# A two-layer attention and expert kernel on one core: in the second attention, the magnitudes' square roots move from ScalarE to VectorE, the ring of exp tiles grows from 8 to 16, and the bias matmuls go in 256-column steps

## The reference, cut to what matters

```python
xn = _layernorm(x, axis=-1)
# attention: heads of 8 channels; the product with v is elementwise,
# so of the softmax only its sums per query are needed
att = jnp.einsum('blhd,bmhd->blmh', q, k) * scale
att = jax.nn.softmax(att, axis=2)
opt = jnp.einsum('blmh,blhd->blhd', att, v).reshape(b, l, d)
attention = opt @ w_out.T + b_out
# "ffn": the magnitudes
real = jnp.einsum('bti,io->bto', xn, jnp.cos(theta + theta_noise))
imag = jnp.einsum('bti,io->bto', xn, jnp.sin(phi + phi_noise))
x = x + attention + jnp.sqrt(real * real + imag * imag)
```

## Time and profile before

| | |
|---|---|
| median of 3 runs | 1477.16 us |
| span of the profiled execution | 1475.7 us |
| what lies around the span (difference) | 1.5 us |
| second attention's stage | 987 us to the end |
| ACT busy | 98% of the span |
| DVE, PE, POOL busy | 84%, 76%, 43% |

### The profile page before, as it was taken

The page is one execution under the profiler, slowest core; times in us unless marked ns, Lnnn a source line. Parts: engine busy times, 40 slices in busy tenths (PEclk is TensorE's granted clock), DMA queues, the critical chain, the costliest instruction groups (busy, mean ns, idle before and its releaser), DMA issues.

```text
span 1475.7 us, 21637 instructions
## 1 busy us (share of the span) xinstructions
PE 1125.2 (76%) x7910; PEld 441.5 (30%) x7910; DVE 1245.1 (84%) x2236; ACT 1445.4 (98%) x796; POOL 632.5 (43%) x529
## 2 busy tenths in 40 slices
PE   5587786887887988878878774787778677776766
PEld 2122223144252441542524411232123122221212
DVE  6998887988989879789798787858898898998886
ACT  3999999999999999999999999999999999999998
POOL 5166460754509577595585820732113023022100
PEclk8599998999999999999999997899999999999999
DMA  4843544213242212122121321034033033021020
GB/s 124 247 137 74 160 128 124 58 52 85 79 136 65 56 43 58 38 56 64 31 66 48 84 68 31 20 108 93 28 117 76 31 110 82 27 106 34 22 72 19
DMA packets 104061, 112.73 MB, mean 76 GB/s; under 512 B 41722, under 2 KB 76026, under 8 KB 103946
## 3 DMA queue, kind: packets, MB, share of 16 engines
q1 hardware_dynamic: 98618, 99.47, 24.5%
q0 software_dynamic: 4464, 11.09, 2.7%
q10 hardware_dynamic: 864, 0.69, 0.2%
HBM read 66.52 MB, written 44.70 MB: 75 GB/s over the span
## 4 chain that ended last, share of the span: by engine, by line
ACT 72%; issue 12%; DVE 11%; PE 3%; POOL 2%; DMA 1%; SPq 0%; ACTq 0%; DVEq 0%; POOLq 0%
ACT scores L785 28%; ACT scores L746 25%; ACT exp L1304 11%; DVE exp L1312 5%; DVE scores L695 4%; ACT exp L1300 2%; ACT ht L1037 1%; ACT L785 1%; ACT L746 1%; POOL yro L1091 1%; PE pvb L676 1%; PE ring L661 1%; ACT scores L778 0%; PE ring L1279 0%; POOL at L1254 0%
## 5 line engine op out<-in xcount | busy, mean ns | idle before, releaser
L695 DVE TENSOR_SCALAR scores<-ring 128x1024 f32<-128x1024 f32 x512 | 589.7, 1216 | 28.7 <-PE ring L661 23.5
L785 ACT ACTIVATE scores<-scores 128x8192 f32<-128x8192 f32 x63 | 438.9, 7020 | 0.2
L1304 ACT ACTIVATE exp<-ring 128x1024 f32<-128x1024 f32 x438 | 432.7, 1419 | 0.2
L746 ACT ACTIVATE scores<-scores 128x8192 f32<-128x8192 f32 (+1 forms) x59 | 404.2, 6919 | 0.2
L1279 PE MATMUL ring<-stk 128*128 128x512 bf16 x1024 | 306.7, 385 | 122.8 <-ACT exp L1304 100.1
L676 PE MATMUL pvb<-scores,val 128*9 128x256 f32 x4096 | 324.6, 392 | 80.6 <-issue 38.4
L1312 DVE SCALAR_TENSOR_TENSOR exp<-exp 128x512 f32<-128x512 f32 x438 | 322.6, 758 | 62.2 <-ACT exp L1304 56.3
L661 PE MATMUL ring<-stk 64*128 64x512 bf16 x1024 | 210.4, 408 | 56.6 <-DVE scores L695 44.5
L1279 PEld LDWEIGHTS ring<-stk 128*128 128x128 bf16 x1024 | 65.8, 97 | 338.3 <-ACT exp L1304 234.4
L661 PEld LDWEIGHTS ring<-stk 64*128 64x128 bf16 x1024 | 49.9, 93 | 288.5 <-DVE scores L695 201.8
L676 PEld LDWEIGHTS pvb<-scores,val 128*9 128x9 f32 x4096 | 65.6, 89 | 210.8 <-issue 207.4
(11 more groups left out here) (263 smaller groups left out, 1415.8 us busy)
## 6 DMA issues: line engine op xcount, KB each, us to landing
stk<-stack SPq DMA_DIRECT2D x192, 192.0 KB, 2.8
stack<-qp SPq DMA_DIRECT2D x7, 768.0 KB, 4.7
stack<-kp SPq DMA_DIRECT2D x7, 768.0 KB, 5.7
xj<-xg SPq DMA_DIRECT2D x10, 448.0 KB
yg<-xj POOLq DMA_DIRECT2D x10, 448.0 KB
stack<-qp SPq DMA_DIRECT2D x7, 512.0 KB, 5.1
stack<-kp SPq DMA_DIRECT2D x7, 512.0 KB, 5.1
stk<-sum_rows SPq DMA_DIRECT2D x128, 24.0 KB
```

Source lines behind the costliest of these rows:

```text
L695: nc.vector.tensor_scalar(S[place][:, j * N:(j + 1) * N], tile, 1e-12, None, ALU.max).then_inc(o.release(("qk", group, place, j)), 1)
L746: nc.scalar.activation(part, part, ACT.Sqrt).then_inc(root_done, 1)
L785: nc.scalar.activation(S[place][:], S[place][:], ACT.Exp, scale=-1.0).then_inc(exp_done, 1)
L1304: nc.scalar.activation(EX[k // 2][:, k % 2, :], tile, ACT.Exp, scale=SCALE1).then_inc(o.release(("qk1", n, i)), 1)
```

## The change

The roots leave ACT. DVE makes them for each batch in six operations over 128x1024 elements, after the folds of s = 4, 8, 14, 66, 70 and 75: an integer multiply and add on the bits of x, a product x*y, its product with y, and a cubic in Horner's form. The ring `EX` has 16 tiles. `add_bias` yields after every 256 columns, so a full bias takes four tiles and not one. `ATURN_AT` goes from 18 to 16, `AWO_AT` from 26 to 22, `FWO_AT` from 36 to 34, `WO_LAST_AT` from 120 to 118; DVE's sums of the projections follow at + 8, not + 4.

```diff
-            EX = [late_room(f"exp{i}", [P, 2, N]) for i in range(NT // 2)]
+            EX = [late_room(f"exp{i}", [P, 2, N]) for i in range(KEPT // 2)]      # KEPT = 2 * NT
+            mag_y, mag_t = late_room("mag_y", [P, N]), late_room("mag_t", [P, N])
...
-            for t in range(0, tokens, 4):
-                n = min(4, tokens - t)
-                nc.tensor.matmul(tile[:, t * P:(t + n) * P].rearrange("p (t c) -> p t c", c=D), ident,
-                                 bcast(late[name], 1, n), start=True, stop=False)
+            for t in range(0, tokens, 2):
+                nc.tensor.matmul(tile[:, t * P:(t + 2) * P].rearrange("p (t c) -> p t c", c=D), ident,
+                                 bcast(late[name], 1, 2), start=(t % 4 == 0), stop=False)
+                yield
...
-            if n:
+            if now >= KEPT:
                 if k % 2 == 0:
-                    act.wait_ge(summed, FOLDS[b * H * NT + s - NT + 2])
+                    act.wait_ge(summed, FOLDS[now - KEPT + 2])
...
+        def dve_magnitudes(dve, chain, b):
+            x, y, t = flat(mag[b]), mag_y[:], mag_t[:]
+            lead, rest = ROOT_CUBIC[0], [c / ROOT_CUBIC[0] for c in ROOT_CUBIC[1:]]
+            dve.wait_ge(mag_half, 2 * (b + 1))
+            if b:
+                dve.wait_ge(mag_root, b)
+            chain.step(nc.vector.tensor_scalar(y.bitcast(I32), x.bitcast(I32), -0.5, ROOT_BITS, ALU.mult, ALU.add))
+            yield
+            chain.wait()
+            chain.step(nc.vector.scalar_tensor_tensor(out=t, in0=x, scalar=lead, in1=y, op0=ALU.mult, op1=ALU.mult))
+            yield
...
+            nc.vector.scalar_tensor_tensor(out=x, in0=x, scalar=rest[2], in1=t, op0=ALU.add, op1=ALU.mult
+                                           ).then_inc(mag_root, 1)
...
-        FTURN_AT, ATURN_AT, AWO_AT, FWO_AT = 10, 18, 26, 36
+        FTURN_AT, ATURN_AT, AWO_AT, FWO_AT = 10, 16, 22, 34
+        MAG_AT = (4, 8, 14, 66, 70, 75)
-        WO_LAST_AT, ADD_LAST_AT = WEIGH_LAST_AT[0] + 8, [H * NT - 6, H * NT - 2]
+        WO_LAST_AT, ADD_LAST_AT = WEIGH_LAST_AT[0] + 6, [H * NT - 6, H * NT - 2]
...
-                        if b == B - 1 and s == MAG_HEAD * NT:
-                            act_magnitudes(act)
...
+                        if s in MAG_AT:
+                            next(magnitudes)
```

More of the change, by code:

```diff
@@ L103 @@
 AUX = 3
+KEPT = 2 * NT
 NEWTON, NEWTON_PLACE = 448, 1
@@ L109 @@
 NEWTON_BITS = 1597463174.0
+ROOT_BITS = 1597475136.0
+ROOT_CUBIC = [-0.311009398570952, 1.309311493198078, -2.1856000529958877, 2.187297202867173]
 PACKS = {
@@ L332, in build @@
         stk1_in = [sem(f"stk1_in{i}") for i in range(GROUP)]
-        mag_root, mag_added, f_added, out_done = (sem("f_" + n) for n in ("mag_root", "mag_added", "added", "out"))
+        mag_steps, mag_root, mag_added, f_added, out_done = (
+            sem("f_" + n) for n in ("mag_steps", "mag_root", "mag_added", "added", "out"))
         g_in, g_s, g_copied, g_root, g_max, g_exp, g_turn, g_pt, g_pv, g_rd, g_att, g_out, g_slot = (
@@ L1120, in pe_project_att @@
             pe.wait_ge(late_in, 48)
-            add_bias(tile, "bo0", NT)
-            yield
+            yield from add_bias(tile, "bo0", NT)
             o.emptied(pe, ("aturn", b))
@@ L1289, in act_exp1 @@
         def act_exp1(act, o, b, s):
-            (n, i), k = tile_at(b, s), s % NT
+            (n, i), now = tile_at(b, s), b * H * NT + s
+            k = now % KEPT
             tile = o.filled(act, ("qk1", n, i))
-            if n:
+            if now >= KEPT:
                 if k % 2 == 0:
-                    act.wait_ge(summed, FOLDS[b * H * NT + s - NT + 2])
+                    act.wait_ge(summed, FOLDS[now - KEPT + 2])
             elif i == 0:
-                act.wait_ge(pv_done, CHG * (GROUPS - 1) + CH)
+                act.wait_ge(pv_done, CHG * (GROUPS - 1) + (n + 1) * CH)
             if sum_by_act(n, i):
@@ L1307, in dve_fold @@
         def dve_fold(dve, o, b, s):
-            (n, i), k = tile_at(b, s), s % NT
+            (n, i), k = tile_at(b, s), (b * H * NT + s) % KEPT
             o.emptied(dve, ("qk1", n, i))
@@ L1352, in pe_project_end @@
             tile = o.begin(pe, ("fwo", b), slot)
-            add_bias(tile, "bo1", NT)
-            yield
+            yield from add_bias(tile, "bo1", NT)
             o.emptied(pe, ("fturn", b))
@@ L1390, in pe_project_last @@
             tile = o.begin(pe, ("fwo", B - 1, number), slot)
-            add_bias(tile, "bo1", hi - lo)
-            yield
+            yield from add_bias(tile, "bo1", hi - lo)
             o.emptied(pe, ("fturn", B - 1, number))
@@ L1417, in act_magnitudes @@
                 nc.scalar.activation(mag[b][:, :, :], mag[b][:, :, :], ACT.Sqrt).then_inc(mag_root, 1)
+        def dve_magnitudes(dve, chain, b):
[9 more added lines that the diff above has]
+            yield
+            chain.wait()
+            chain.step(nc.vector.scalar_tensor_tensor(out=y, in0=t, scalar=1.0 / lead, in1=y, op0=ALU.mult,
+                                                      op1=ALU.mult))
+            yield
+            chain.wait()
+            chain.step(nc.vector.scalar_tensor_tensor(out=x, in0=y, scalar=rest[0], in1=y, op0=ALU.add, op1=ALU.mult))
+            yield
+            chain.wait()
+            chain.step(nc.vector.scalar_tensor_tensor(out=x, in0=x, scalar=rest[1], in1=y, op0=ALU.add, op1=ALU.mult))
+            yield
+            chain.wait()
+            nc.vector.scalar_tensor_tensor(out=x, in0=x, scalar=rest[2], in1=t, op0=ALU.add, op1=ALU.mult
+                                           ).then_inc(mag_root, 1)
+            yield
         def pool_add_magnitudes(pool, o, b, after_end):
@@ L1540, in build @@
         LAST_OUT_AT, LAST_TURN_AT, LAST_DIVIDE_AT = 10, 14, 13
-        FTURN_AT, ATURN_AT, AWO_AT, FWO_AT = 10, 18, 26, 36
+        FTURN_AT, ATURN_AT, AWO_AT, FWO_AT = 10, 16, 22, 34
         ADD_AT, STATS1_AT, NORMAL_AT, TURN1_AT = 31, 47, 57, 68
         Q1_AT, K1_AT, SPLIT1_AT, V1_AT, MIX_AT = 79, 88, (92, 94, 96, 98), 97, (108, 120)
-        MAG_HEAD, STORE1_HEAD, STORE_RESULT_HEAD = 2, 12, 6
+        MAG_AT = (4, 8, 14, 66, 70, 75)
+        STORE1_HEAD, STORE_RESULT_HEAD = 12, 6
         WEIGH_LAST_AT = [LAST_GROUP + GROUP * hi for _, hi in LAST_PARTS[:-1]]
         TURN_LAST_AT, KEEP_LAST_AT = [WEIGH_LAST_AT[0] + 4, H * NT - 2], [WEIGH_LAST_AT[0] + 5, H * NT - 4]
-        WO_LAST_AT, ADD_LAST_AT = WEIGH_LAST_AT[0] + 8, [H * NT - 6, H * NT - 2]
+        WO_LAST_AT, ADD_LAST_AT = WEIGH_LAST_AT[0] + 6, [H * NT - 6, H * NT - 2]
         def at_once(steps):
@@ L1730, in fast @@
                                 project_end = pe_project_end(pe, o, b - 1, AUX)
-                            if FWO_AT <= s < FWO_AT + 5:
+                            if FWO_AT <= s < FWO_AT + 8:
                                 next(project_end)
@@ L1741, in fast @@
                                 project_att = pe_project_att(pe, o, b + 1, AUX)
-                            if AWO_AT <= s < AWO_AT + 5:
+                            if AWO_AT <= s < AWO_AT + 8:
                                 next(project_att)
@@ L1772, in fast @@
                                 project_last = pe_project_last(pe, o, 0, AUX)
-                            if WO_LAST_AT <= s < WO_LAST_AT + 5:
+                            if WO_LAST_AT <= s < WO_LAST_AT + 6:
                                 next(project_last)
@@ L2268, in fast @@
                     dve_divide(dve, GROUPS - 1, place)
+                mag_chain = Chain(dve, mag_steps)
                 for b in range(B):
+                    magnitudes = dve_magnitudes(dve, mag_chain, b)
                     for s in range(H * NT):
@@ L2279, in fast @@
                                 dve_keep_att(dve, o, b + 1)
-                            if s == AWO_AT + 4:
+                            if s == AWO_AT + 8:
                                 dve_add_att(dve, o, b + 1)
@@ L2305, in fast @@
                             dve_keep_end(dve, o, b - 1)
-                        if b and s == FWO_AT + 4:
+                        if b and s == FWO_AT + 8:
                             dve_add_end(dve, o, b - 1)
```

## The result

| | median of the timed runs, us | runs | ratio to before, 95% interval |
|---|---|---|---|
| before | 1477.88 (1476.40 to 1479.67) | 11 | |
| changed | 1480.15 (1478.88 to 1482.48) | 11 | 1.0018 (1.0010 to 1.0026) |
| changed, timed again on another chip (before there: 1477.57) | 1479.20 (1476.76 to 1480.48) | 11 | 1.0011 (1.0002 to 1.0020) |

The account below looks back on a forecast made before the run. ACT, busy 98% of the span, was taken to set the pace. -7.5 + 3.0 + 1.4 + 1.6 = -1.5 us gave 1475.7, plus 0.6 for the clock: 1476.3 us; 8-in-10 range 1471.5 to 1480.3.

Parts of the forecast that it names:

- I put in 0.6 for all four together: Sum: allowance in us for PE's clock falling to 1.2 GHz at the four stops, added to 1475.7.
- What is removed, 7.5 us: On ACT: roots and both tables 6.5 us, late exps at biases 0.8, bias near the end about 0.25.
- What DVE gets, 0.69 + 5 x 1.22: On DVE: six root operations, 6.8 us per batch, fitting in batch 1's 13.3 us of idle.
- What would show it: Signs in the profile: no root or table rows, exps late at s = 17, idle PE, DVE busy 27 us longer.
- Four stops, where and why: PE waits at s = 16 in batch 0 (load) and 1, 2 (DVE's copy), and at batch 3's end (copy).
- Their sizes, 1.4, 1.5, 1.5 and 1.6: Us lost on ACT: 1.4 in batch 0, 1.5 each in batches 1 and 2, 1.6 at batch 3's end.
- The measure: Taken from a late exp at a bias: an exp for which PE is late ends 1.65 us after its scores start.
- 0 to 1.4 us: Clock price per stop: first exp 0.9 us later at 1.2 GHz, second transposes up to 0.5 more.
- the idle of 2.17 us that kept the clock and the one of 2.53 that lost it: PE idles in the earlier profile, clock 1.00 and 0.50 after them; stops of about 2.4 to 2.6 us lie between.
- slower, by the clock: Rival: each of the four stops drops PE's clock to 1.2 GHz, 4 x 1.4 us, giving 1481.3 us; chance 0.13.
- the stops are not hidden: Against the rival that PE's wait for `aux` doesn't bind and the whole 7.5 us shows, 1469.7 us; chance 0.17.
- POOL's additions do stretch folds: Rival: DVE's root operations collide with POOL's additions, 2 us more lost in batches 1 and 2, 1478.3; chance 0.06.

Follow-up runs that it names:

- Roots later: The changed kernel with the first three root operations after the folds of s = 20, 24 and 28, not 4, 8 and 14: 1473.78 us, ratio 0.9977 to before.
- places alone: The kernel before (roots on ACT, ring of 8) with only the split bias, earlier places and DVE's sums at + 8: 1481.36 us, ratio 1.0029.
- the end's place back: The changed kernel with the last projection begun at s = 120 again, not 118, bias still split: 1476.79 us, ratio 0.9997 to the kernel before.

## Why the prediction was wrong

The step that failed is the last one of the sum: "I put in 0.6 for all four together." The clock cost 4.7 us; the terms ahead of it in the sum came out within 0.2 us each.

- *What is removed, 7.5 us.* Measured 6.62 for the roots and 1.06 for the biases, 7.7.
- *What DVE gets, 0.69 + 5 x 1.22.* Right. In the changed kernel the first operation takes 0.75 us in the mean and the others 1.22 to 1.23, and batch 1 shows no idle of ACT that comes from them when the places are those of before. DVE's busy time grew by 23.8 us and not by the 27 that "What would show it" names, since each operation overlaps its neighbours by about 0.15 us. The multiply on integer bits runs near the conversion's 0.69 us, not near 1.22; the row, with minimum, median and maximum:

```profile
L1433 DVE TENSOR_SCALAR mag_y<-mag x4: 683/748/809, 992.9 to 1364.9; 128x1024 int32<-128x1024 int32 x4
```

- *Four stops, where and why.* Right in all four: batches 1 and 2 for DVE's copy behind two root operations, batch 0 for the load, the end for the copy behind s = 117. "Roots later", "places alone" and "the end's place back" each took away just the stops that this mechanism gives them.
- *Their sizes, 1.4, 1.5, 1.5 and 1.6.* With the clock kept up they are 1.41, 1.50, 1.52 and 1.75. The measure (an exp ends 1.65 us after the scores start) holds as long as the clock does; in the changed kernel's batch 1, with the clock down, it is 1126.91 + 1.02 - 1125.81 = 2.12 us.
- *The clock.* In the changed kernel the stops cost 2.26, 3.12, 2.39 and 3.10 us. Less the above that is 0.85, 1.62, 0.87 and 1.35 us, 4.7 in all. The price for one stop, "0 to 1.4 us", was worked out well, too low only for batch 1, where the first exp lost 0.89 and the second transposes cost 0.73, not 0.5. What I got wrong is how often: I took the idle of 2.17 us that kept the clock and the one of 2.53 that lost it as two bounds and valued the four at 0.6, under half of one full dip. The idles came out as foreseen, at 2.34, 2.37, 2.37 and 2.56 us, and the clock fell at every stop. They lie at the middle between the two rows, near the upper one or above it, so an even chance for each would have been the least that the rows allowed: 4 x 0.5 x 1.4 = 2.8 us, and a forecast of 1478.5. The reading itself was too narrow: the idle's length as the one thing that decides. At one length, 2.56 us, the runs show both outcomes.
- *The rival that came true* is "slower, by the clock" (1481.3 us, chance 0.13): 1475.7 + 4.7 = 1480.4, measured 1480.15. That this lies inside the stated range, which ends at 1480.3, is luck: the lateness alone gives 1480.4. Of the others, the stops are not hidden, and POOL's additions do stretch folds at the start of batch 3, but the ring of 16 takes that up.

Open is what makes the same 2.56 us at the same place cost the clock in one kernel and not in another. The changed kernel on a second chip lost it at the same four stops (at 1002.8, 1122.2, 1245.1 and 1460.2 us, its first exp 1.6 us earlier), at the same moments behind its first exp within 0.01 us. But "the end's place back", the same program up to the end of batch 3, had its falls 0.95 us later, and where the fall comes later behind a stop, the stop costs another amount. So what a stop costs isn't settled by the stop alone. The Trainium skill ("TensorE: Matmul & The Clock Gate", What's actually happening) calls the window over which the activity is watched free-running, not reset by the kernel, and has the moment of the clock's rise depend on where in it the first matmul lands. Falls that shift as a whole between executions of one program agree with that, and so does the pair of equal idles; but no run here varied only this, so that it decided the fall is not shown.

## What to carry to other kernels

A step that is moved earlier so that another fits asks for its inputs and its buffer earlier; if these don't come earlier too, the move turns slack into a stop of the engine, as the split bias did here, worth 1.1 us and paid with 10.9 us of stops. Where a stop of PE would be nearly as long as one in the same trace that cost the clock, price the stop with the clock down, and look for useful work to lay into it: even useless work paid here (3.3 us). Take the parts of a change apart before judging it: the roots on VectorE with the ring of 16 are worth 7 us, and the second projection's bias was worth splitting where it could begin at its old place (the first one's was not tried there).

## What the hardware did that I had not expected

An idle of PE of 2.34 us was enough for 1.2 GHz behind it, 0.84 us after PE had begun again, and one of 2.56 us was not always, after the same work: 1.22 us for two bias matmuls in one kernel, 0.70 in another. The falls kept their distances from each other but came 0.95 us later, against the first exp, in one execution than in another of a program that is the same up to there. In batch 1 the clock was still down when the second transposes came at s = 19 (0.50 over the 6 us shown), and they cost 0.73 us more; in batch 2 they cost nothing. Two POOL additions stretched two folds from 0.68 to 2.83 and 2.82 us, each to the length of one addition, wherever they fell.
